# Aggregation loops of a graph network on one NeuronCore: where the comparison row lies, who stages the gather indices, and how finely the engines wait

## The reference

```
def _gcn_layer(x, src, dst, norm, W, b, n_nodes):
    h = x @ W
    msg = h[src] * norm[:, None]
    out = jax.ops.segment_sum(msg, dst, num_segments=n_nodes)
    return out + b
...
x = _gcn_layer(x_piece, src, dst, norm, W1, b1, n_nodes)
x = jax.nn.gelu(x)
x = _gcn_layer(x, src, dst, norm, W2, b2, n_nodes)
x = jax.nn.gelu(x)
x = _gcn_layer(x, src, dst, norm, W3, b3, n_nodes)
```

## Time and profile before

| what | us |
|---|---|
| median of 3 runs | 14757.23 |
| profiled execution, span from the first to the last instruction | 14933.7 |
| first part: sorting, tables, first normalisation | 0 to 1904 |
| three aggregations, loops with their drain | about 2494, 2500 and 2473 |
| three `finish` stages | about 277 each |
| attention layer (gathers of another table) | about 10200 to 13500 |
| experts | about 13500 to 14934 |

### The profile page before, as it was taken

The page is one execution under the profiler, slowest core; times in us unless marked ns, Lnnn a source line. Parts: engine busy times, 40 slices in busy tenths (PEclk is TensorE's granted clock), DMA queues, the critical chain, the costliest instruction groups (busy, mean ns, idle before and its releaser), DMA issues. The chain is left out here.

```text
span 14933.7 us, 122356 instructions
## 1 busy us (share of the span) xinstructions
PE 6795.4 (46%) x29462; PEld 5570.3 (37%) x29462; DVE 6207.0 (42%) x12229; ACT 2112.3 (14%) x6085; POOL 7853.7 (53%) x8847
## 2 busy tenths in 40 slices
PE   0120034333434334343443334336555555777999
PEld 0120023333323333333333333325333334777888
DVE  8870233333333333333333333335444445553222
ACT  0000000000001000000100000003666664111222
POOL 0387367777765777777477777761545554330000
PEclk9997566676667666666666666666555555558999
DMA  0000133333322333333133333323000000001000
GB/s 8 7 0 5 44 103 88 88 88 88 89 68 73 89 87 88 88 87 88 53 88 90 90 88 90 88 65 94 5 5 5 5 5 4 1 1 33 28 29 27
DMA packets 468304, 809.55 MB, mean 54 GB/s; under 512 B 156361, under 2 KB 306425, under 8 KB 468210
## 3 DMA queue, kind: packets, MB, share of 16 engines
q0 software_dynamic: 309248, 667.09, 16.3%
q1 hardware_dynamic: 158962, 141.56, 3.1%
HBM read 729.01 MB, written 79.15 MB: 54 GB/s over the span
## 5 line engine op out<-in xcount | busy, mean ns | idle before, releaser
L691 POOL DMA_INDIRECT work<-feature_table,stage x4992 | 5155.3, 1033 | 1758.4 <-issue 1575.6
L708 PE MATMUL ps<-work,onehot 128*128 128x256 f32 x9984 | 2933.4, 465 | 5150.6 <-DVE onehot L719 2591.1
L708 PEld LDWEIGHTS ps<-work,onehot 128*128 128x128 f32 x9984 | 2367.5, 241 | 5716.4 <-issue 5274.2
L734 DVE TENSOR_TENSOR acc<-acc,ps 128x256 f32 x4992 | 2103.8, 421 | 4472.5 <-PE ps L708 1772.9
L1052 PE MATMUL ps<-ident,onehot 128*128 128x128 f32 x4608 | 1160.9, 402 | 1105.1 <-ACT onehot L1037 435.8
L1037 ACT ACTIVATE onehot<-work 128x128 f32<-128x128 bf16 x4608 | 1374.5, 387 | 801.8 <-DMA HG<-L_ffn_edge_index_in 635.4
L1052 PEld LDWEIGHTS ps<-ident,onehot 128*128 128x128 f32 x4608 | 767.6, 204 | 1498.1 <-issue 770.9
L1018 POOL DMA_INDIRECT work<-attention_table,stage x1152 | 1106.3, 960 | 405.3 <-issue 349.8
L226 POOL DMA_INDIRECT edge_list<-rec_stage,stage x1024 | 1115.7, 1090 | 369.2 <-issue 309.5
L780 ACT ACTIVATE work<-acc,dinv 128x256 f32 (+1 forms) x294 | 131.6, 496 | 7732.1 <-PEq L794 7539.5
L1075 DVE TENSOR_REDUCE work<-ps 128x4 f32<-128x512 f32 x1152 | 720.6, 684 | 885.0 <-DMA HG<-L_ffn_edge_index_in 652.6
(11 more groups left out here) (202 smaller groups left out, 5302.9 us busy)
## 6 DMA issues: line engine op xcount, KB each, us to landing
work<-feature_table,stage POOLq DMA_INDIRECT x4992
feature_table<-acc SPq DMA_DIRECT2D x98, 256.0 KB
work<-attention_table,stage POOLq DMA_INDIRECT x1152
edge_list<-rec_stage,stage POOLq DMA_INDIRECT x1024
feature_table<-acc SPq DMA_DIRECT2D x7, 1792.0 KB, 6.7
x_after_gnn<-acc SPq DMA_DIRECT2D x49, 256.0 KB
x_normed_t<-work SPq DMA_DIRECT2D x49, 256.0 KB, 2.2
acc<-x_normed_t SPq DMA_DIRECT2D x49, 256.0 KB, 2.8
```

The costliest lines, as they stand in the source:

```text
L691: nc.gpsimd.indirect_dma_start(out=ring[:, h, k], out_offset=None, in_=table, in_offset=bass.IndirectOffsetOnAxis(ap=stage[:, h, k:k + 1], ...
L708: mm = nc.tensor.matmul(ps[:, bank, (k % 2) * D:(k % 2 + 1) * D], onehot[:, h, k], ring[:, h, k], start=True, stop=True, skip_group_check= ...
L734: nc.vector.tensor_tensor(acc[:, at], acc[:, at], ps[:, bank, (k % 2) * D:(k % 2 + 1) * D], ALU.add).then_inc(s_add, 1)
```

## The change

It rewrites `aggregate` and adds a small block ahead of it.

- `iota` is copied once into bank 7 of PSUM (`iota_ps`), and the comparison of `hots` reads it from there; `dloc` stays in SBUF.
- ACT copies the index columns into one of four stages (`stage4`, made of `stage` and `rec_stage`), up to four halves ahead. POOL no longer copies; it waits for `s_stg` and `s_used` and then issues the 16 gathers.
- There is a row semaphore for each four gathers, and PE waits for four gathers ahead of each four products, no longer for 16 ahead of 16.
- The products use the PSUM banks 0 to 3 alone: 8 places, two groups of four.
- DVE makes the comparison matrices of half m+1 ahead of the adds of half m.
- A turn of the loops has four halves, 26 turns a layer; on DVE the last turn is written out.

```diff
+        iota_ps = ps[:, 7, 0:P]
+        stage4 = [stage[:, 0], stage[:, 1], rec_stage[:, 0], rec_stage[:, 1]]
+        with nc.Block() as block:
+            @block.vector
+            def _(dve):
+                nc.vector.tensor_copy(iota_ps, iota[:]).then_inc(s_ips, 1)
+                dve.wait_ge(s_ips, 1)
...
-            s_row = [sem(f"rows_in{h}" + n) for h in range(2)]
+            s_row = [[sem(f"rows_in{h}{j}" + n) for j in range(QH)] for h in range(2)]
...
+                @block.scalar
+                def _(act):
+                    def put(m, r):
+                        nc.scalar.copy(stage4[r], idx[0][:, bass.ds(m * U, U)]).then_inc(s_stg, 1)
+                    for m in range(4):
+                        put(m, m)
+                    with act.Fori(0, LAPS - 1) as g:
+                        for r in range(4):
+                            act.wait_ge(s_row[r % 2][QH - 1], g * (32 * Q) + (r // 2 + 1) * (16 * Q))
+                            put(g * 4 + (4 + r), r)
...
-                            pool.wait_ge(s_used, g * 2 + (h + 1))
-                            pool.sem_inc(s_tick, 1)
-                            nc.gpsimd.tensor_copy(stage[:, h], idx[0][:, bass.ds(g * (2 * U) + h * U, U)]).then_inc(s_stg, 1)
-                            pool.wait_ge(s_stg, g * 2 + (h + 1))
-                            pool.sem_inc(s_tick, 1)
+                    def gather(m, r):
+                        pool.wait_ge(s_stg, m + 1)
+                        pool.sem_inc(s_tick, 1)
+                        pool.wait_ge(s_used, m + 1)
+                        pool.sem_inc(s_tick, 1)
+                        for k in range(U):
+                            nc.gpsimd.indirect_dma_start(
+                                out=ring[:, r % 2, k], out_offset=None, in_=table,
+                                in_offset=bass.IndirectOffsetOnAxis(ap=stage4[r][:, k:k + 1], axis=0),
+                            ).then_inc(s_row[r % 2][k // Q], 16)
...
-                            pe.wait_ge(s_row[h], (g + 1) * (16 * U))
-                            pe.wait_ge(s_hot, g * 2 + (h + 1))
+                    pe.sem_inc(s_sum, 2)
+                    def products(m, r, lap):
+                        pe.wait_ge(s_hot, m + 1)
+                        for k in range(U):
+                            q = k // Q
+                            if k % Q == 0:
+                                pe.wait_ge(s_sum, m * QH + (q + 1))
+                                pe.wait_ge(s_row[r % 2][q], lap * (32 * Q) + (r // 2 + 1) * (16 * Q))
+                            mm = nc.tensor.matmul(ps[:, 2 * (q % 2) + (k % Q) // 2, (k % 2) * D:(k % 2 + 1) * D],
+                                                  onehot[:, r % 2, k], ring[:, r % 2, k],
+                                                  start=True, stop=True, skip_group_check=True)
...
-                            onehot[:, h], iota[:].unsqueeze(1).broadcast_to([P, U, P]),
+                            onehot[:, r % 2], iota_ps.unsqueeze(1).broadcast_to([P, U, P]),
...
+                    hots(0, 0)
+                    with dve.Fori(0, LAPS - 1) as g:
+                        for r in range(4):
+                            dve.wait_ge(s_used, g * 4 + (r + 2))
+                            hots(g * 4 + (r + 1), (r + 1) % 4)
+                            adds(g * 4 + r, r)
```

More of the change, by code:

```diff
@@ L669, in build @@
         ring = work[:].rearrange("p (h u f) -> p h u f", h=2, u=U)
-        G1 = S1 // (2 * U)
+        HV = S1 // U
+        LAPS = HV // 4
         Q = 4
+        QH = U // Q
+        iota_ps = ps[:, 7, 0:P]
+        stage4 = [stage[:, 0], stage[:, 1], rec_stage[:, 0], rec_stage[:, 1]]
+        s_ips = sem("iota_in_psum")
+        assert HV % 4 == 0 and U % Q == 0
+        with nc.Block() as block:
[3 more added lines that the diff above has]
+                dve.wait_ge(s_ips, 1)
         def aggregate(l):
             n = f"_l{l}"
-            s_row = [sem(f"rows_in{h}" + n) for h in range(2)]
+            s_row = [[sem(f"rows_in{h}{j}" + n) for j in range(QH)] for h in range(2)]
             s_stg, s_tick = sem("indices_staged" + n), sem("pool_tick" + n)
@@ L678, in aggregate, with halves @@
             s_hot, s_mm, s_add, s_sum = sem("onehots" + n), sem("products" + n), sem("adds" + n), sem("psum_free" + n)
+            def halves(eng, body):
+                with eng.Fori(0, LAPS) as g:
+                    for r in range(4):
+                        body(g * 4 + r, r)
             with nc.Block() as block:
+                @block.scalar
[8 more added lines that the diff above has]
+                            put(g * 4 + (4 + r), r)
@@ L680, in _ @@
                 @block.gpsimd
                 def _(pool):
-                    with pool.Fori(0, G1) as g:
-                        for h in range(2):
-                            pool.wait_ge(s_used, g * 2 + (h + 1))
-                            pool.sem_inc(s_tick, 1)
-                            nc.gpsimd.tensor_copy(stage[:, h], idx[0][:, bass.ds(g * (2 * U) + h * U, U)]).then_inc(s_stg, 1)
-                            pool.wait_ge(s_stg, g * 2 + (h + 1))
-                            pool.sem_inc(s_tick, 1)
[L690 to L694, removed]
+                    def gather(m, r):
[8 more added lines that the diff above has]
+                            ).then_inc(s_row[r % 2][k // Q], 16)
@@ L696, in _ @@
+                    halves(pool, gather)
                 @block.tensor
@@ L698, in _ @@
                     pe.sem_inc(s_used, 2)
-                    with pe.Fori(0, G1) as g:
-                        for h in range(2):
-                            pe.wait_ge(s_row[h], (g + 1) * (16 * U))
-                            pe.wait_ge(s_hot, g * 2 + (h + 1))
[L703 to L713, removed]
+                    pe.sem_inc(s_sum, 2)
@@ new lines, in products @@
+                    def products(m, r, lap):
[8 more added lines that the diff above has]
+                                                  start=True, stop=True, skip_group_check=True)
+                            if k % Q == Q - 1:
+                                mm.then_inc(s_mm, 1)
+                        pe.wait_ge(s_mm, m * QH + QH)
+                        pe.sem_inc(s_used, 1)
@@ L715, in _, with hots @@
+                    with pe.Fori(0, LAPS) as g:
+                        for r in range(4):
+                            products(g * 4 + r, r, g)
                 @block.vector
                 def _(dve):
-                    dve.sem_inc(s_sum, U // Q)
-                    def hots(g, h):
+                    def hots(m, r):
                         nc.vector.tensor_tensor(
-                            onehot[:, h], iota[:].unsqueeze(1).broadcast_to([P, U, P]),
-                            dloc[0][:, bass.ds(g * (2 * U) + h * U, U)].unsqueeze(2).broadcast_to([P, U, P]),
+                            onehot[:, r % 2], iota_ps.unsqueeze(1).broadcast_to([P, U, P]),
+                            dloc[0][:, bass.ds(m * U, U)].unsqueeze(2).broadcast_to([P, U, P]),
@@ L722, in hots, with adds @@
                             ALU.is_equal).then_inc(s_hot, 1)
[L723 to L739, removed]
-                        dve.sem_clear(s_add)
+                    def adds(m, r):
+                        for k in range(U):
+                            q = k // Q
+                            if k % 8 == 0:
+                                base = load_blocks(mybir.EngineType.DVE, 0, m * U + k, top=(NB - 1) * D)
+                            if k % Q == 0:
+                                dve.wait_ge(s_mm, m * QH + (q + 1))
+                            at = bass.ds(base[k % 8], D)
+                            nc.vector.tensor_tensor(
+                                acc[:, at], acc[:, at],
+                                ps[:, 2 * (q % 2) + (k % Q) // 2, (k % 2) * D:(k % 2 + 1) * D], ALU.add).then_inc(s_add, 1)
+                            dve.wait_ge(s_add, r * U + k + 1)
+                            if k % Q == Q - 1:
+                                dve.sem_inc(s_sum, 1)
@@ new lines, in _ @@
+                    hots(0, 0)
+                    with dve.Fori(0, LAPS - 1) as g:
+                        for r in range(4):
+                            dve.wait_ge(s_used, g * 4 + (r + 2))
+                            hots(g * 4 + (r + 1), (r + 1) % 4)
+                            adds(g * 4 + r, r)
+                        dve.sem_clear(s_add)
+                    for r in range(4):
+                        m = (LAPS - 1) * 4 + r
+                        if r < 3:
+                            dve.wait_ge(s_used, m + 2)
+                            hots(m + 1, r + 1)
+                        adds(m, r)
```

## The result

The changed kernel took 15487.14 us (median of 4 runs, 15484.65 to 15502.89) where the kernel before took 14764.65 us: ratio 1.0488, 95% interval 1.0473 to 1.0503. It is 4.9% slower where 6.8% faster was forecast. The experiments show that this holds only in some measuring sessions; in another the same change is 5.8% faster.

What follows compares the result with a forecast made beforehand. POOL's gathers were taken to bound the loops; -419 - 291 - 345 - 23 + 4 = -1074 us from the 14933.7 us span gave 13860. Allowing for the lower median, the forecast was 13755 us, range 13650 to 13880 (0.66).

Steps and rivals of the forecast that it cites:

- What bounds the kernel: Aggregation loops: POOL's gathers set the pace, 23.7 us a half, of which the change can reach 3.7 us.
- The row in PSUM: Onehots in the loops: reading the row from PSUM stops them lengthening POOL's gathers, saving 419 us.
- Index copies on ACT: Staging in the loops: moving POOL's index copies to idle ACT saves 291 us.
- item 3: POOL's waits in the loops for PE's release of the ring, 344.7 us, all expected to go.
- item 2: Staging on POOL in the loops: index copies and the longer pause before the next gather, 291 us, expected to go.
- released about 8 us after the half's last gather: Ring in the loops: the last group's place is free by then, while POOL wants it 20 us after.
- that group q+2 finds the adds of group q done: PSUM ring of 8: adds finish 3.9 + 2.4 us after group q's rows; group q+2's rows come 10 us after.
- a sign that the forecast is wrong: Changed profile's loops: POOL waiting over 50 us in all for PE's release of the ring would refute the forecast.
- two rivals: Loops: PE becomes the bound, about 14130 us, chance 0.15; late releases meet the small PSUM ring, about 15650, chance 0.04.
- the one that came nearest: PSUM ring of 8: late releases for each group make a half 26.6 us, about 15650 us in all; chance 0.04.
- Span and median: Whole kernel: median lies 176.5 us below the profiled span; the forecast was set between 13683 and 13860 us.

Runs made afterwards that it cites:

- clean session: Measuring session in which the kernel before takes 13382 to 13392 us and no profile has a group late by the stricter measure.
- run with ACT's copies: Kernel before with only the index copies moved from POOL to ACT: 14763.35 us, 0.9981 of before.
- late session: Measuring session in which the kernel before takes 14765 to 14939 us and products are released late wherever POOL's gathers feed them.
- run with the ring alone: Kernel before with only its PSUM product places cut from 16 to 8: 14804.21 us, 1.0009 of before.
- late run with SP's transfers: Changed kernel with SP's plain DMAs of 128 fixed rows replacing POOL's gathers in the loops, where before takes 14939.40 us: 11481.35 us.

## Why the prediction was wrong

**What bounds the kernel: half right.** "So POOL sets the pace" holds for the changed kernel in a clean session, where a loop takes 2096 us from its first onehot to its last add. In the late ones a loop goes by POOL and by PE's late releases together. The 291 us off POOL in the run with ACT's copies gained 30, which a kernel paced by POOL could not do.

**The row in PSUM: right in mechanism, wrong in what it frees.** Gathers fell to 947 ns as forecast. In the clean session it is worth 491 us (419 forecast; in the new order every onehot lengthens a gather: 312 over 1.2 us, 256 in the kernel before). In a late session it costs 287 us against the run with the ring alone (15091.32 against 14804.21). The inference that the Trainium skill makes ("SBUF — State Buffer", section "Who interferes with whom"), that such a `tensor_tensor` would not stall a DMA issued by POOL, has the traces against it once more: the mean is 1031 to 1044 ns in all versions with the row in SBUF and under 951 ns in all with it in PSUM.

**Index copies on ACT, and item 3.** In clean sessions everything but the row is worth 289 us (13383.62 to 13094.99), about the 291 of item 2 alone. That fits the absence of item 3's 345 us there; no profile of before was taken in such a session, so this is not seen directly. The whole gain there is 780 us, the forecast without item 3 is 729. In the late sessions item 3 did not go, it grew to 1814 us.

**The step that failed** is "Item 3, 344.7 us, goes", with its covers: that the last place is "released about 8 us after the half's last gather", and that group q+2 finds the adds of group q done. Both used PE's records (3.9 us a group). The release seen by DVE was the number to use, and the 1652.7 us of remote waits stood beside it. In its place the runs showed reports that DVE awaits idle for 4104 us in all and up to 19 us at a time, and 1814 us of waits by POOL, where over 50 us was named as a sign that the forecast is wrong.

I left these to two rivals, and excused the one that came nearest (0.04, about 15650 us; measured 15487) by "they come once a half, at the end of a burst of 16". In number that was nearly so: in the kernel before DVE stood idle behind 350 groups, 219 of them the fourth of a half and 98 the third, though 658 had their adds over 1.2 us behind. What failed is that it read the lateness as a property of the burst. It goes with POOL's issuing: in the changed kernel groups 1 and 2 of a half are late by 8.4 and 12.9 us on average, groups 3 and 4, which make up 257 of the 274 in a pause of POOL, by 4.4 and 2.2. Nor is it the ring alone, as that rival had it: the ring of 8 cost the old order nothing. That its number came near is in part luck: it took 7 us as the lateness at 2451.19, where the rows give 8.3, and with 8.3 its own sum is 29.2 us a half and about 16460 us; measured was 25.9 us a half.

Ring and row in PSUM together are the step from 0.989 to 1.049 of before (14629 and 15487 us, two late sessions). How it divides between them in the new order is open, as the version with row in SBUF and ring of 8 met clean sessions three times.

**Span and median.** I set 72 of the 176.5 us between them to the loops. Medians of before in late sessions range from 14765 to 14939 us; the gap may be that of two sessions and no part of the loops, but no run shows which.

**What holds PE's release is not settled.** Two more signs go with it. The first is in the records. A gather leaves 16 completion records. The traces of the clean sessions have 121331 such records of all DMAs (the version with row in SBUF) and 121336 (the changed kernel), those of the late ones 41818 (before), 30329 and 29801 (the changed kernel): about two thirds or more are missing, with all 4992 gathers and all packets there. In the late run with SP's transfers none is missing in the three loops (79872), while before the first loop 7108 stand where a clean session has 11326.

The second is that not PE alone is held. In the first part of the kernel a loop on DVE (line 565 on) does register work and two small instructions in each turn and waits for no other engine, while POOL scatters the other graph's edges with indirect DMAs. A register instruction of line 565 (shortest, median and longest duration in ns) and the copies of some turns, in the late profile of the changed kernel:

```profile
L565 DVEq ALU_OP  x98: 10/40/1396, 1289.9 to 1666.1; - x98
...
1398.84 0.18 DVE L571 COPY idx<-acc  x1 [11.07 <-issue]
...
1412.73 0.18 DVE L571 COPY idx<-acc  x1 [12.14 <-issue]
```

and in its clean one:

```profile
L565 DVEq ALU_OP  x98: 40/40/40, 1290.4 to 1473.1; - x98
...
1398.02 0.18 DVE L571 COPY idx<-acc  x1 [1.43 <-issue]
...
1399.87 0.20 DVE L571 COPY idx<-acc  x1 [1.44 <-issue]
```

In the late profile a turn takes 14 us where it takes 1.85, its register instructions starting 0.7 us apart or a multiple of that, until POOL pauses at 1531.4; from 1536 on a turn takes 1.85 us again. Every late profile has 125 to 135 of these instructions over 0.3 us, out of 785, and no clean one has any. So a theory in which PE alone is disturbed, by its reading or its bursts, is too narrow. Instructions that come at even distances while records are missing would fit a recording that cannot keep up and holds the engines; whether it does, and whether the late time would be there without it, was not tried.

## What to carry to other kernels

Before counting time taken off the busiest engine as gained, look at how late the releases of its partner are: compare the partner's last record with the start of the instruction it releases, not with its own durations. If a remote wait of many us stands there, shorter work on the first engine can turn into waiting or even cost time, and an edit that also takes buffers away between the two (here 8 PSUM places of 16) needs a run of its own. And time the kernel before in more than one session: the version with 16 places and the row in SBUF gained in both kinds (1.1% and 2.2%), the whole change won 5.8% in one and lost 4.9% in the other.

## What the runs showed of the hardware that I had not expected

- The same kernel takes 13384 or 14794 us depending on the session, both given as chip 14. In the profiles of the changed kernel the difference lies where POOL issues indirect DMAs: the span up to the first loop is 1670 or 1893 us, a loop 2096 or 2697, the `finish` stages between the loops, in which POOL scatters too, 176 or 277, the attention layer from its first to its last gather 1624 or 2149, and the experts, with no such DMA, 1359 in both.
- A completion is not lost with its record, and DMA completions are not late: ACT's index copies, which wait for the rows of a half, start 1.8 to 2.0 us after the end of its last gather in the late profile and 1.8 to 2.1 us in the clean one (2427.20 after a gather issued at 2424.33 in the changed kernel's trace), while PE's reports are up to 30 us late.
- A DVE loop that waits for nothing of POOL's was slowed too while POOL issued indirect DMAs: 14 us a turn where it takes 1.85, in late sessions alone.
